# GNN layer pair: places double-buffered, running counts in SBUF, scatters by half groups with a wait in the middle

## The chip, the cores and the metric

One core of a Trainium2 chip runs the whole program. The metric is the device time of one launch in microseconds, without a profile. The kernel before has a median of 7398.5 us over three runs. A profile is taken in an execution of its own, which is slower: see the section on the profile.

## The reference

Two graph layers over 12500 nodes of 128 features and 212500 directed edges (`src`, `dst`, sorted by `dst`), each followed by a residual and a layer norm:

```python
# layer 0
h = silu(edge_attr @ W1 + b1)
messages = x[dst] * (h @ W2 + b2)
aggregated = segment_sum(messages, src, 12500)
x = layernorm(x + concat(x @ Wself + bself, aggregated) @ Wcat + bcat)
# layer 1
a_in  = mean over dst of (x @ W_in.T + b_in)[src]
a_out = mean over src of (x @ W_out.T + b_out)[dst]
x = layernorm(x + gru_cell(concat(a_in, a_out), x))
```

In layer 0 the messages are made in the order of `dst` and summed by `src`. The kernel therefore sorts them: it works out for each edge its place in the order of `src`, and scatters each message to its row of the DRAM tensor `msgs`.

## The kernel before

Edges are worked on in 208 groups of 1024 (`NG` = 208, `GE` = 1024), each group as `TG` = 8 tiles of 128. After a preamble (144.3 us in the trace) the edge phase runs over the groups in pairs (`b` = 0, 1 are the two buffers of a pair); then `sums0` adds up the scattered messages by blocks, the first layer norm follows, and then layer 1 with 3322 gathers of 128 rows each (L757), issued by GpSimd; last comes the GRU cell with the second norm.

The edge phase is the stage that the change touches. Every engine has its own instruction stream with waits on semaphores written by hand. In group g:

- SP (L475 to L494) loads rows of keys, attributes and a window of x.
- PE: for both halves of the group, the neighbours' rows by a one-hot product (`neighbours`, L1827) for g, the hidden layer (`hidden`, L1820) and the transposed attributes (`attributes`, L1814) for g+1. Then `places(g)` (L1836): eight products of `place` with a column of ones, which give the place of each edge, into `places_at`, a strip of PSUM bank 7. Then `weights` (L1842, L1844) in two halves, and the first half of the attributes of g+2, ahead of which PE waits for `pos_ready`, that is until DVE has copied the places of g; the attributes share bank 7 with the places.
- DVE: one-hots of the source digit (L1337) and the attribute parts (L1364 to L1367) of a later group, then for g+1 the running counts by a scan (`running_counts`, L1344) into `so_far`, which is PSUM bank 6, and the product of counts and one-hots (`places_of`, L1351) into `place` in SBUF, each twice, once per half, with the window's one-hots (L1373) between. `place` has one buffer, so the first product waits until PE's `places(g)` is done (`place_ready`). Then DVE copies the places of g to `pos` (L1398; it waits for `place_ready` and for the scatters of g-2) and multiplies weights and neighbours to messages, in two halves (L1379), into `mrow`.
- ACT: copies out of PSUM (L856, L858, L870), the activation (L864) and the two key columns of `mrow` (L886, L887).
- GpSimd (`scatters`, L697): waits for `pos_ready`, `key_ready` and both halves of `msg_ready`, and then issues eight indirect DMAs, one per tile, of 128 rows of 544 bytes, from `mrow` to `msgs`. `mrow` and `pos` have two buffers; the semaphores `scattered[b]` count the landings, 16 per DMA.

`Steps.wait` (L65) is a wait of DVE for its own last instruction; `hold` (L85, L86) is a wait of GpSimd and a nop behind it.

Of the kernel before, what the change touches and what calls it, by code (L numbers as in the profile page):

```python
# [8 lines left out]
P = 128  # L9
TG = 8  # L10
GE = TG * P
NG = -(-E // GE)
# [76 lines left out]
def gnn_kernel(nc, x, src, dst, edge_attr, W1, b1, W2, b2, Wself, bself, Wcat, bcat,  # L89
# [24 lines left out]
    with ctx:  # L114
# [85 lines left out]
        ht = cut(2 * 2 * 4 * P).rearrange("p (b h e) -> p b h e", b=2, h=2)  # L200
        place = cut(GE)
        attr_t = cut(GE, bf16)
        ustage = acc_b[:, 2 * QE + T:2 * QE + T + 3 * SB * D].rearrange("p (h n d) -> p h n d", h=3, n=SB)
        xpart_x = cut(D)
        xpart_t = cut(P)
        xpart_sb = cut(D)

        cut = cutter(arena, STAGE)
# [129 lines left out]
        bank = [ctx.enter_context(nc.psum_tensor(f"bank{i}", [P, 512], f32)) for i in range(8)]  # L338
        so_far = bank[6][:, :]
        attr_at = bank[7][0:W1R, 0:2 * P].bitcast(bf16)  # L340
        places_at = bank[7][:, 2 * P:2 * P + TG]
        xpart_at = bank[7][:, 2 * P + TG:3 * P + TG]

# [286 lines left out]
        def _(pool):  # L630
# [59 lines left out]
            def scatters(it):  # L690
                for b in range(2):
                    g = 2 * it + b
                    hold(pool, s["pos_ready"], g + 1)
                    hold(pool, s["key_ready"], 2 * g + 2)
                    hold(pool, s["msg_ready"], 2 * g + 2)
                    for j in range(TG):
                        pool.indirect_dma_start(msgs, bass.IndirectOffsetOnAxis(ap=pos[:, b, j:j + 1], axis=0), mrow[:, b, j, :], None).then_inc(scattered[b], 16)  # L697

# [374 lines left out]
        def _(dve):  # L1073
# [272 lines left out]
            def places_of(stp, g, b, h):  # L1346

                stp.wait()
                need(dve, s["place_ready"], 0 if h else g)
                half = oht[:, b, 4 * h:4 * h + 4, :].rearrange("p j e -> p (j e)")  # L1350
                stp.mark(v.tensor_tensor(place[:, h * 4 * P:(h + 1) * 4 * P], so_far, half, ALU.mult))  # L1351
                if h:
                    stp.wait()
                    dve.sem_inc(s["place_in"], 1)
# [70 lines left out]
            v.tensor_copy(blk0_f, blk0[:, :]).then_inc(s["blk0_copied"], 1)  # L1425
            v.memset(acc_a[:, :], 0.0)
            us.link(v.tensor_copy(node_at, iota_row[:, :]))
            def onehot0(q, k):
# [260 lines left out]
        def _(pe):  # L1689
# [111 lines left out]
            def attributes(g, b, h, nb=None):  # L1801

                pe.wait_ge(s["attr_cut"], g + 1)
                need(pe, s["attr_sb"], 2 * g + h)
                if h == 0:
                    need(pe, s["pos_ready"], g - 1)
                if nb is not None and b:
                    mm(xpart_at, ones_b[0:3, :], bias3[:, :], start=True, stop=False)
                    mm(xpart_at, xpart_t, wcomb[:, :], start=False, stop=True)
                elif nb is not None:  # L1810
                    pe.wait_ge(x_staged[0], nb * 16 + 16)
                    tr(xpart_at, xpart_x, ident[:, :])
                for k in range(4):
                    last = tr(attr_at[:, k * P:(k + 1) * P], attr_p[:, b, 4 * h + k, :, :].rearrange("p k c -> p (k c)"), ident_b[:, :])  # L1814
                last.then_inc(s["attr_tr"], 1)
# [14 lines left out]

            def places(g):

                pe.wait_ge(s["place_in"], g + 1)
                need(pe, s["pos_ready"], g)
                for j in range(TG):
                    last = mm(places_at[:, j:j + 1], place[0:NBP, j * P:(j + 1) * P], ones[0:NBP, 0:1], start=True, stop=True)  # L1836
                last.then_inc(s["place_ready"], 1)
# [9 lines left out]
            def edge_group(it, more=True, nb=None):  # L1847
                for b in range(2):
# [9 lines left out]
                    if then:  # L1858
                        hidden(g + 1, 1)
                    places(g)  # L1860
                    for h in range(2):
# [147 lines left out]
```

## Time and profile before

| | |
|---|---|
| median of 3 runs (lowest, highest) | 7398.5 us (7398.36, 7406.37) |
| profiled execution, its own span | 9306.0 us, granted TensorE clock 0.655 |
| edge phase in it, first to last scatter | 3255.0 us |
| first to last gather in it | 5002.2 us |
| GpSimd busy | 5138.4 us of the span |
| PE, DVE, ACT busy | 4988.0, 3928.4, 1905.1 us |

The span runs from the first to the last instruction of the profiled execution; the runs of the first line have no profile. A timeline row of GpSimd's DMA_INDIRECT shows how long the engine works on issuing the DMA, not its landing. In brackets behind a row stands how long the engine was idle before it and what ended that; "issue" means that no wait was found, "remote" that a semaphore's update ended the wait whose origin the profile doesn't find among the instructions near it. Ends of matmuls are modelled.

### The profile page before, as it was taken

The page shows a single profiled execution, that of the slowest core. Times are in us where ns is not written, and L with a number is a line of the kernel's source. Part 1 is how long each engine was busy: PE and PEld are TensorE (multiplying, and loading weights), DVE is VectorE, ACT ScalarE, POOL GpSimd, SP SyncE. Part 2 cuts the span into 40 slices and gives each one's busy share as a digit, 9 for nine tenths or more (in the row PEclk, how much of TensorE's full clock was granted, in tenths as well). Part 3 has the DMA queues.
Part 4 walks back from the last instruction along what each step waited for, and adds up shares of the span by engine and source line. Part 5 has one row for each costly group of instructions (what it writes and reads, how often), then busy time and mean ns, then how long its engine had stood idle before and what let it go on. Part 6 is the DMA issues. An engine that isn't in the chain of part 4 may idle for free. (4 is left out here: it accounts for less than half of the span.)

```text
span 9306.0 us, 123877 instructions
## 1 busy us (share of the span) xinstructions
PE 4988.0 (54%) x25826; PEld 4200.2 (45%) x25826; DVE 3928.4 (42%) x9767; ACT 1905.1 (20%) x6476; POOL 5138.4 (55%) x5753
## 2 busy tenths in 40 slices
PE   5777777767677778833323333333344444434438
PEld 4666666666666668823222232222232333222334
DVE  6444444444445467743222242232332222222238
ACT  2222222222222210021111111111121111111117
POOL 2454544444445455554666666666556666666651
PEclk7666666666666679966555555555576666666668
DMA  3222222222222248731222212222122222222224
GB/s 101 80 84 77 82 78 78 75 76 77 78 75 82 81 141 229 232 94 34 46 46 47 46 41 46 47 46 46 39 53 60 60 60 61 60 59 60 61 67 147
DMA packets 947495, 711.24 MB, mean 76 GB/s; under 512 B 602499, under 2 KB 811606, under 8 KB 946622
## 3 DMA queue, kind: packets, MB, share of 16 engines
q0 software_dynamic: 163632, 347.28, 12.5%
q1 hardware_dynamic: 245634, 251.14, 8.9%
q10 hardware_dynamic: 538001, 110.77, 6.2%
q14 instruction: 205, 1.68, 0.1%
q8 instruction: 23, 0.38, 0.0%
HBM read 544.79 MB, written 170.29 MB: 77 GB/s over the span
## 5 line engine op out<-in xcount | busy, mean ns | idle before, releaser
L757 POOL DMA_INDIRECT arena<-x1d,edge x3322 | 3147.5, 947 | 1859.2 <-issue 957.7
L1937 PE MATMUL bank<-arena 128*128 x7040 | 1433.8, 381 | 2159.8 <-DVE acc_b L1585 1129.5
L697 POOL DMA_INDIRECT msgs<-arena x1664 | 1618.8, 973 | 1761.4 <-DVE arena L1379 1290.2
L1937 PEld LDWEIGHTS bank<-arena 128*128 128x128 f32 x7040 | 1310.9, 285 | 2354.6 <-issue 2345.0
L1579 DVE TENSOR_TENSOR arena<-bank,arena 128x1024 f32<-128x1024 f32 x440 | 537.5, 1222 | 2518.7 <-remote 2182.8
L987 ACT ACTIVATE arena<-edge,arena 128x1 f32 x3520 | 730.3, 282 | 2600.0 <-issue 2021.4
L1351 DVE TENSOR_TENSOR acc_b<-bank,arena 128x512 f32<-128x512 f32 x416 | 287.6, 691 | 1474.5 <-remote 1368.0
L1585 DVE TENSOR_TENSOR acc_b<-acc_b,bank 128x129 f32 x1760 | 507.2, 288 | 661.5 <-issue 467.3
L1844 PE MATMUL bank<-w2s,acc_b 128*128 128x128 f32 x3328 | 739.6, 392 | 0.0
L1827 PE MATMUL bank<-arena 128*128 (+1 forms) x3328 | 729.1, 389 | 1.0 <-DVE arena L1373 0.6
L1844 PEld LDWEIGHTS bank<-w2s,acc_b 128*128 128x128 f32 x3328 | 628.9, 282 | 134.9 <-issue 134.9
L1827 PEld LDWEIGHTS bank<-arena 128*128 128x128 f32 x3328 | 663.1, 295 | 2.1 <-issue 1.1
L1585 DVE TENSOR_TENSOR acc_a<-acc_a,bank 128x129 f32 x1760 | 507.2, 288 | 280.0 <-issue 82.0
L1891 PE MATMUL bank<-arena 128*128 128x128 f32 x3712 | 500.1, 300 | 86.4 <-DVE acc_a L1450 63.3
L1344 DVE TENSOR_TENSOR_SCAN bank<-arena,bank 128x512 f32<-128x512 bf16 x415 | 535.4, 1290 | 7.3
L1891 PEld LDWEIGHTS bank<-arena 128*128 128x128 f32 x3712 | 487.8, 203 | 98.7 <-DVE acc_a L1450 69.2
L1923 PE MATMUL bank<-auxw,arena 9*128 9x512 bf16 x98 | 56.2, 574 | 860.6 <-ACT arena L981 837.9
L856 ACT ACTIVATE acc_b<-bank 128x128 f32<-128x128 f32 x196 | 54.3, 277 | 2031.5 <-PE bank L1814 1838.3
L1836 PEld LDWEIGHTS bank<-ones,acc_b 99*128 99x128 f32 x3328 | 454.3, 211 | 11.3
L1836 PE MATMUL bank<-ones,acc_b 99*128 99x1 f32 x3328 | 425.3, 257 | 0.0
L1923 PEld LDWEIGHTS bank<-auxw,arena 9*128 9x128 bf16 x98 | 9.6, 98 | 879.5 <-ACT arena L981 854.7
L713 POOL TENSOR_SCALAR arena<-iota_row,arena 128x128 f32<-128x128 f32 x464 | 273.3, 601 | 195.8 <-PE bank L1891 195.2
(310 smaller groups left out, 5591.1 us busy)
## 6 DMA issues: line engine op xcount, KB each, us to landing
arena<-rows SPq DMA_DIRECT2D x208, 512.0 KB
arena<-msgs ACTq DMA_DIRECT2D x464, 136.0 KB, 3.2
arena<-msgs SPq DMA_DIRECT2D x464, 136.0 KB, 3.0
arena<-x1d,edge POOLq DMA_INDIRECT x3322
msgs<-arena POOLq DMA_INDIRECT x1664
pred<-arena ACTq DMA_DIRECT2D x98, 256.0 KB
arena<-pred SPq DMA_DIRECT2D x12, 1792.0 KB, 8.8
arena<-xwin SPq DMA_DIRECT2D x208, 64.0 KB
```

The costliest lines, as they stand in the source:

```text
L697: pool.indirect_dma_start(msgs, bass.IndirectOffsetOnAxis(ap=pos[:, b, j:j + 1], axis=0), mrow[:, b, j, :], None).then_inc(scattered[b], 16)
L757: pool.indirect_dma_start(grow_t[:, sl, 0:D], None, x1d, bass.IndirectOffsetOnAxis(ap=edge2[:, odd * RING + sl, 1:2].bitcast(i32), axis=0) ...
L987: last_key = nc.scalar.activation(key_now[:, slot, k:k + 1], edge2_f[:, bass.ds(of[k], 1)], ACT.Identity, bias=blk_now[:, slot, k:k + 1])
L1344: stp.mark(v.tensor_tensor_scan(so_far, half, before_it.to_broadcast([P, 4 * P]), before_it, ALU.add, ALU.max))
L1351: stp.mark(v.tensor_tensor(place[:, h * 4 * P:(h + 1) * 4 * P], so_far, half, ALU.mult))
L1579: v.tensor_tensor(oh1[:, q % 2], node_at.rearrange("p (o n) -> p o n", o=1).to_broadcast([P, TG, P]), key_now[:, slot, q * TG:(q + 1) * TG ...
L1585: v.tensor_tensor(a, a, sum_at(q, k), ALU.add).then_inc(s["add1_done"], 1)
L1827: last = mm(bank[4 + h][:, k * P:(k + 1) * P], wsel[:, b, j, :], win[:, b, bass.ds(wide * j, 1), :].rearrange("p o d -> p (o d)"), start=T ...
L1836: last = mm(places_at[:, j:j + 1], place[0:NBP, j * P:(j + 1) * P], ones[0:NBP, 0:1], start=True, stop=True)
L1844: last = mm(bank[2 + h][:, k * P:(k + 1) * P], ht[:, b, h, k * P:(k + 1) * P], w2s[:, :], start=False, stop=(k == 3))
L1891: last = mm(bank[k % 4][:, 0:P], mtile[:, k % S0, i, 0:D], oh0[:, k % SO, i, :], start=(i == 0), stop=(i == 1))
L1937: last = mm(sum_at(q, k), oh1[:, q % 2, k, :], grow[:, bass.ds(rows_at[q * TG + k], CW)], start=True, stop=True)
```

## The change

`place` gets a second buffer, so that DVE's product for g+1 waits for the places of g-1 (`place_ready` at least g, no longer g+1). `so_far` moves from PSUM bank 6 to SBUF, `places_at` moves from bank 7 to bank 6, and PE's wait for `pos_ready` ahead of the attributes goes (the one in `places` stays). GpSimd issues the first four scatters of a group when the first half of the messages is there; before the fifth it waits for the second half and then until the group's first four scatters have landed. A wait of DVE for the last `pos_ready` is added once, behind the loop, before bank 6 is written for other use.

```diff
@@ -198,12 +198,13 @@
 
         cut = cutter(acc_b[:, 2 * QE + T:NBP * CW], NBP * CW - 2 * QE - T)
         ht = cut(2 * 2 * 4 * P).rearrange("p (b h e) -> p b h e", b=2, h=2)
-        place = cut(GE)
+        place = cut(2 * GE).rearrange("p (b e) -> p b e", b=2)
         attr_t = cut(GE, bf16)
         ustage = acc_b[:, 2 * QE + T:2 * QE + T + 3 * SB * D].rearrange("p (h n d) -> p h n d", h=3, n=SB)
         xpart_x = cut(D)
         xpart_t = cut(P)
         xpart_sb = cut(D)
+        so_far = cut(4 * P)
 
         cut = cutter(arena, STAGE)
         S0, SO = NS, 8
@@ -336,10 +337,9 @@
         part_sum = sb("part_sum", [P, 2, LO])
 
         bank = [ctx.enter_context(nc.psum_tensor(f"bank{i}", [P, 512], f32)) for i in range(8)]
-        so_far = bank[6][:, :]
         attr_at = bank[7][0:W1R, 0:2 * P].bitcast(bf16)
-        places_at = bank[7][:, 2 * P:2 * P + TG]
-        xpart_at = bank[7][:, 2 * P + TG:3 * P + TG]
+        places_at = bank[6][:, 0:TG]
+        xpart_at = bank[7][:, 2 * P:3 * P]
 
 
         names = """pads_oh0 pool_const edges_in weights_in dve_step pe_weights act_weights dve_weights aux_in
@@ -692,8 +692,11 @@
                     g = 2 * it + b
                     hold(pool, s["pos_ready"], g + 1)
                     hold(pool, s["key_ready"], 2 * g + 2)
-                    hold(pool, s["msg_ready"], 2 * g + 2)
                     for j in range(TG):
+                        if j % 4 == 0:
+                            hold(pool, s["msg_ready"], 2 * g + 1 + j // 4)
+                        if j == 4:
+                            hold(pool, scattered[b], it * (16 * TG) + 16 * 4)
                         pool.indirect_dma_start(msgs, bass.IndirectOffsetOnAxis(ap=pos[:, b, j:j + 1], axis=0), mrow[:, b, j, :], None).then_inc(scattered[b], 16)
 
             with pool.Fori(0, NG // 2) as it:
@@ -1346,9 +1349,9 @@
             def places_of(stp, g, b, h):
 
                 stp.wait()
-                need(dve, s["place_ready"], 0 if h else g)
+                need(dve, s["place_ready"], 0 if h else g - 1)
                 half = oht[:, b, 4 * h:4 * h + 4, :].rearrange("p j e -> p (j e)")
-                stp.mark(v.tensor_tensor(place[:, h * 4 * P:(h + 1) * 4 * P], so_far, half, ALU.mult))
+                stp.mark(v.tensor_tensor(place[:, b, h * 4 * P:(h + 1) * 4 * P], so_far, half, ALU.mult))
                 if h:
                     stp.wait()
                     dve.sem_inc(s["place_in"], 1)
@@ -1424,6 +1427,7 @@
             dve.wait_ge(s["dlist_out"], 16)
             v.tensor_copy(blk0_f, blk0[:, :]).then_inc(s["blk0_copied"], 1)
             v.memset(acc_a[:, :], 0.0)
+            dve.wait_ge(s["pos_ready"], NG)
             us.link(v.tensor_copy(node_at, iota_row[:, :]))
             def onehot0(q, k):
                 v.tensor_tensor(oh0[:, (4 * q + k) % SO], node_at.rearrange("p (o n) -> p o n", o=1).to_broadcast([P, 2, P]),
@@ -1802,8 +1806,6 @@
 
                 pe.wait_ge(s["attr_cut"], g + 1)
                 need(pe, s["attr_sb"], 2 * g + h)
-                if h == 0:
-                    need(pe, s["pos_ready"], g - 1)
                 if nb is not None and b:
                     mm(xpart_at, ones_b[0:3, :], bias3[:, :], start=True, stop=False)
                     mm(xpart_at, xpart_t, wcomb[:, :], start=False, stop=True)
@@ -1828,12 +1830,12 @@
                               win[:, b, bass.ds(wide * j, 1), :].rearrange("p o d -> p (o d)"), start=True, stop=True)
                 last.then_inc(s["xj_ready"], 1)
 
-            def places(g):
+            def places(g, b):
 
                 pe.wait_ge(s["place_in"], g + 1)
                 need(pe, s["pos_ready"], g)
                 for j in range(TG):
-                    last = mm(places_at[:, j:j + 1], place[0:NBP, j * P:(j + 1) * P], ones[0:NBP, 0:1], start=True, stop=True)
+                    last = mm(places_at[:, j:j + 1], place[0:NBP, b, j * P:(j + 1) * P], ones[0:NBP, 0:1], start=True, stop=True)
                 last.then_inc(s["place_ready"], 1)
 
             def weights(g, b, h):
@@ -1857,7 +1859,7 @@
                     neighbours(g, b, 1)
                     if then:
                         hidden(g + 1, 1)
-                    places(g)
+                    places(g, b)
                     for h in range(2):
                         weights(g, b, h)
                     if more:
```

## Rows read from the trace of the kernel before

**Rows 1.** The page's head: span of the profiled execution and its instructions.

```profile
span 9306.0 us, 123877 instructions
```

**Rows 2.** Windows: edge phase and gathers; columns PE, PEld, DVE, ACT, POOL busy, clock, DMA.

```profile
core 0: us, PE busy (x) PEld busy (x) DVE busy (x) ACT busy (x) POOL busy (x), PEclk, DMA share, GB/s
...
144.30:3399.30 3255.00, 2369.82 (x12793) 2045.79 (x12791) 1562.79 (x2677) 781.68 (x1847) 1618.81 (x1664) 0.64 0.24 79
...
4038.10:9040.30 5002.20, 1805.13 (x7856) 1452.37 (x7856) 1543.32 (x3995) 875.24 (x3834) 3147.51 (x3322) 0.61 0.22 52
```

**Rows 3.** Waits of GpSimd: line, releaser, us in total, times, longest in us.

```profile
POOL msgs L697 <- DVE arena L1379: 1290.2, 207, 125.2
POOL arena L757 <- issue: 957.7, 3140, 0.9
POOL arena L757 <- remote: 663.3, 164, 5.5
POOL msgs L697 <- issue: 470.0, 1453, 2.2
POOL arena L757 <- PE bank L1937: 233.6, 17, 90.6
```

**Rows 4.** Waits in the edge phase, same columns: DVE's place product.

```profile
DVE acc_b L1351 <- remote: 1368.0, 175, 8.9
```

**Rows 5.** Timeline of GpSimd, one group's scatters and the next group's first.

```profile
start us, us, engine line op out<-in xcount [idle before <-releaser]
1502.09 0.97 POOL L697 DMA_INDIRECT msgs<-arena  x1 [6.94 <-DVE arena L1379]
1503.36 0.97 POOL L697 DMA_INDIRECT msgs<-arena  x1 [0.30 <-issue]
1504.63 1.02 POOL L697 DMA_INDIRECT msgs<-arena  x1 [0.30 <-issue]
1505.96 0.97 POOL L697 DMA_INDIRECT msgs<-arena  x1 [0.30 <-issue]
...
1511.04 0.97 POOL L697 DMA_INDIRECT msgs<-arena  x1 [0.30 <-issue]
1518.85 0.97 POOL L697 DMA_INDIRECT msgs<-arena  x1 [6.84 <-DVE arena L1379]
```

**Rows 6.** Timeline of DVE in the same stretch.

```profile
1502.45 0.36 DVE L1367 TENSOR_TENSOR arena<-arena 128x192 bf16<-128x192 f32 x1
...
1503.92 0.89 DVE L1373 TENSOR_SCALAR arena<-arena,iota_c 128x1024 f32<-128x1024 bf16 x1
1513.62 0.69 DVE L1351 TENSOR_TENSOR acc_b<-bank,arena 128x512 f32<-128x512 f32 x1 [8.81 <-remote]
...
1516.59 0.17 DVE L1398 CAST arena<-bank 128x8 int32<-128x8 f32 x1 [0.22 <-DVE acc_b L1351]
1516.78 1.29 DVE L1379 TENSOR_TENSOR arena<-bank,arena 128x512 f32<-128x512 f32 x2
```

**Rows 7.** Timeline of PE in the same stretch: places and the second weights.

```profile
1505.84 1.94 PE L1836 MATMUL bank<-ones,acc_b 99*128 99x1 f32 x16
...
1509.42 2.07 PE L1844 MATMUL bank<-w2s,acc_b 128*128 128x128 f32 x8
```

**Rows 8.** Timeline at the edge phase's end: last scatter, first load behind all scatters.

```profile
3398.33 0.96 POOL L697 DMA_INDIRECT msgs<-arena  x1 [0.31 <-issue]
3400.80 1.42 ACTq L918 DMA_DIRECT2D arena<-msgs  x3
```

**Rows 9.** Timeline around a gap in a group's scatters, DVE and GpSimd.

```profile
347.83 0.17 DVE L1398 CAST arena<-bank 128x8 int32<-128x8 f32 x1 [0.24 <-DVE acc_b L1351]
...
353.29 0.97 POOL L697 DMA_INDIRECT msgs<-arena  x1 [2.23 <-issue]
...
355.36 0.69 DVE L1351 TENSOR_TENSOR acc_b<-bank,arena 128x512 f32<-128x512 f32 x1 [2.70 <-PE bank L1836]
...
358.33 0.17 DVE L1398 CAST arena<-bank 128x8 int32<-128x8 f32 x1 [0.22 <-issue]
```

## The prediction, made before the changed kernel was run

> **What bounds the kernel now.** I read the profile in this order: the span, the split of GpSimd's time by stretch, GpSimd's waits, and then one turn of the edge loop engine by engine. The profiled execution spans 9306.0 us [rows 1]; the runs without a profile have a median of 7398.5 us. The two differ by 1907.5 us, so before any cost is added up the reader has to ask which of the waits in the trace exist in the timed runs at all.
>
> The edge loop takes 3255.0 us for 208 groups (15.65 us each), and the gathers 5002.2 us [rows 2]. In both GpSimd issues indirect DMAs one after another. GpSimd's waits account for its edge time exactly: 1618.8 us busy, 470.0 us of gaps between DMAs ("issue"), and 1290.2 us of waiting for the messages, of which 125.2 us is one wait ahead of the loop, so 1165.0 us inside [rows 2, 3]. In the gathers it waits 663.3 us for something that the profile can't name, and 233.6 us for PE, of which 90.6 us in one place [rows 3].
>
> Where the 1165.0 us come from is to be seen in one turn. GpSimd issues the eight scatters of a group at 1.27 us a piece, the first at 1502.09 and the last at 1511.04 [rows 5]. PE's records end early: the products that give the places (L1836) start at 1505.84 and last 1.94 us, the second half of the message products starts at 1509.42 and lasts 2.07 us [rows 7]. Yet DVE's place product (L1351), which needs the semaphore of exactly that L1836, starts only at 1513.62 after 8.81 us of idling [rows 6], 2.58 us after the last scatter began. In 175 groups DVE so waits, 1368.0 us in all [rows 4]. PE's completions thus come late while GpSimd issues, and everything behind them (counts, places, messages, the next scatters at 1518.85) goes in a row. The Trainium skill (Perfetto Trace Analysis, "Per-instruction lifecycle: what the profiler-reported window actually captures") says that a matmul's end is computed from its size, not observed. So the record's end doesn't contradict the late semaphore; no term below rests on this.
>
> Do the timed runs have those waits? Take away from the profiled span the 1165.0 us and the 663.3 us: 7477.7 us. The median is 79.2 us less still, which is 0.016 us for each of the 4986 indirect DMAs. I read from this that in the timed runs GpSimd hardly waits, and that the late completions belong mostly to the profiled execution. Then a group costs GpSimd (1618.8 + 470.0) / 208 = 10.04 us, and GpSimd sets the pace. One caution: a turn without the late completion took 358.33 - 347.83 = 10.50 us from one copy of the places to the next [rows 9], a little over 10.04. So PE and DVE in turn are nearly as slow, and PE's busy time is 2369.8 / 208 = 11.4 us a group at a granted clock of 0.64 [rows 2], mostly the 1.2 GHz level. In the timed runs they must be near or under GpSimd's 10.04 or the median couldn't be that low.
>
> **The change part by part.** The sum is made per group, times 208, and put onto the median, since the profiled execution has waits that I hold to be its own.
>
> *The place buffer twice, counts in SBUF, places in a bank of their own.* DVE's product for group g+1 now needs the places of g-1 and not of g; PE's attribute transposes no longer wait for the copy of the places (pos_ready). In the turn shown this takes product, scan and product out of the path, from 1513.62 to 1516.59, 2.97 us [rows 6]. Where GpSimd is the bound this is worth nothing: what is late next is GpSimd itself. Queued behind the copy on DVE are the two message products, as before. The work added is none; DVE has 1562.8 / 208 = 7.5 us of work per group [rows 2], so a few hundredths from another source or destination memory lie beside GpSimd's scatters. Bounds: 0 and -2.97 us per group.
>
> *A rule that speaks against it.* The product now reads the counts from SBUF, as well as the one-hots. The existing product of two SBUF inputs, L1367 (1502.45, 0.36 us), ran while the scatter of 1502.09 was being issued, and that scatter took 0.97 us like its neighbours; the conversion L1373 (1503.92), with one input, is the one beside which a scatter took 1.02 us [rows 5, 6]. The Trainium skill (SBUF — State Buffer, "Who interferes with whom") says that a DVE instruction with two SBUF inputs contends with a GpSimd instruction that reads SBUF. By the row the cost is 0. By the rule, if it blocked the scatters for the two products of 0.69 us, it would be 1.38 us per group, 287 us in all; the trace doesn't show it.
>
> *Scatters by half groups.* The first four need only the first half of the messages. DVE makes the two halves in 1.29 us together from 1516.78 [rows 6], so the first four may start some 0.6 us earlier when GpSimd waits for messages. When GpSimd is the bound: 0. Bounds 0 and -0.6 us.
>
> *The fifth scatter waits until the first four have landed.* This is the term that counts. GpSimd's queue is in order: behind the wait stand scatters five to eight and the whole next group. It can't be free: the fourth scatter alone is at work for 0.97 us, and the next began 1.27 us after its start [rows 5]. What the trace shows of landing: the last scatter started at 3398.33, and the first load that waits for all scatters was issued at 3400.80, 2.47 us later [rows 8]. From the wait's end to a scatter's start: the second message product ended at 1516.78 + 1.29 = 1518.07, the scatter began at 1518.85, 0.78 us later [rows 5, 6]. Together 3.25 us from fourth to fifth start; from below it is 0.97 + 0.78 = 1.75. Against the usual 1.27 that is 1.98 or 0.48 us more. I take 1.7, close to the upper end, because 2.47 is the same DMA and the same kind of wait, less some tenths for the loading engine's own first instruction. Nothing on GpSimd covers it. What can is only slack that the group has now, if PE and DVE at 10.50 and not GpSimd at 10.04 set the pace: I take 0.3 us off for that, more than half of the difference.
>
> Sum: 208 x (1.7 - 0.3) = 291 us, 7398.5 + 291 = 7690 us. A group goes from 10.04 to about 11.7 us, and that is also above PE's 11.4. The profiled execution may well go the other way: with a pause in a train of scatters PE's completions came in time. After the gap of 2.23 us ahead of the scatter of 353.29 DVE's product ran at 355.36 already, on a wait of 2.70 us [rows 9]. There the group would fall from 15.65 to some 12.3 us and the span to about 8600 us.
>
> **The rivals.**
>
> *The pause is covered.* If PE's clock in the timed runs is as low as in the trace, PE's 11.4 us is the pace now. The indirect DMAs must then be shorter for the median to come out: by (79.2 + 208 x 1.36) / 4986 = 0.073 us, a train 9.45 us. With the pause 11.15 us, still under 11.4; with the waits of PE on DVE gone, the gain is 0 to 0.3 us a group: 7340 to 7400 us, and up to 7600 with half the slack. For it: PE's busy time. Against: it needs shorter DMAs than any row.
>
> *The late completions are in the timed runs too.* This is the case on the other side. The 957.7 and 470.0 us of "issue" gaps [rows 3] might be the profiler's instead; without them the span is 7878 us, so 480 of the 1828 us of waits would be gone and 1349 stay, of which the edge loop's share 860 us, 4.1 us a group. Then the change pays: 2.97 + 0.6 us leave the path, 1.7 come in, -1.9 us x 208 = -390 us: about 7010 us; if the pause also lets PE's completions through, down to 6800. It decides from 1.7 us of wait per group on. For it: waits are measured, the gap's origin isn't. Against: it needs all 0.30 us gaps to vanish, where the other reading meets the median within 1%.
>
> *More than the pause.* Landing at the full 1.98 us with no slack is 412 us, 7810 us; with the rule of the ports above (a chance of 0.02) near 8000.
>
> That the change doesn't do what it says is excluded: a fourth scatter that works for 0.97 us can't have landed when the fifth is due after 0.30.
>
> **How the numbers follow.** Forecast 0.54 (7600 to 7790); pause covered 0.18, a third each faster, equal and slower; late completions real 0.18; more than the pause 0.10. A measurement of this kernel can tell about 0.2% (15 us) from no change. Faster: 0.18 + 0.06 = 0.24; same 0.06; slower 0.54 + 0.10 + 0.06 = 0.70. The forecast's own range is 7600 to 7790. To hold 8 in 10 the range takes in the covered pause, the near end of the gain and the exposed pause in full: 7250 to 7820.
>
> **What would show it.** In the changed kernel's trace: the fifth scatter (L697's successor) starts about 3.0 us after the fourth, the others 1.27; if under 2, my main term is wrong. DVE's product no longer waits for PE; in its place the copy of the places or the message products wait. PE's completion is late in fewer groups and by less. The edge stretch is near 2560 us, the other stretches are unchanged. A scatter over 1.0 us beside L1351 would speak for the port rule. If the median falls by over 15 us, the reading that the timed runs have no GpSimd waits is wrong, and with it the sum.

## The result and the profile after

| | before | changed | ratio, 95% interval |
|---|---|---|---|
| first comparison, median | 7398.43 us | 7797.49 us | 1.0542 [1.0529, 1.0555] |
| second, chip 11 | 7382.4 us | 7799.31 us | 1.0566 [1.0548, 1.0584] |
| third, chip 10 | 7390.66 us | 7804.93 us | 1.0555 [1.0533, 1.0577] |

The change makes the kernel 5.5% slower, 399 us in the first comparison. It was predicted as slower, 7690 us, with a range of 7250 to 7820 us. (For the first comparison the record gives no number of the chip.)

One thing has to be known to understand every number below. The kernel before runs in two ways, and all its runs on one chip went the same way: in 7382 to 7398 us (medians) in three comparisons, in 9254 to 9331 us in three others. The trace ahead of the prediction (9306.0 us) is of the second kind, the times beside it are of the first. I call the chips quick and late; whether it is the chip, or a state that it was in at the time, isn't known. A comparison is always made within one chip.

The changed kernel's profiled execution spans 7803.8 us, and its time was 7805.69 us: it was on a quick chip, and its time is within 0.3% of the other three runs (7784.22 to 7797.62 us), so the trace describes the timed runs; being traced costs next to nothing, other than the section on the metric says. The windows, by stage (columns as in [rows 2]: PE, PEld, DVE, ACT, POOL busy, clock, DMA); edge phase, sums and norm, gathers, end:

```profile
145.30:2798.40 2653.10, 2271.79 (x12789) 1972.87 (x12786) 1537.55 (x2680) 804.49 (x1847) 1735.70 (x1664) 0.72 0.29 96
2798.40:3438.70 640.30, 545.87 (x3908) 523.40 (x3908) 496.11 (x1958) 45.49 (x100) 326.87 (x711) 0.91 0.76 223
3438.70:7601.30 4162.60, 1870.70 (x8048) 1604.27 (x8048) 1597.96 (x4105) 829.58 (x3914) 3150.05 (x3322) 0.64 0.28 62
7601.30:7803.80 202.50, 171.96 (x718) 98.95 (x718) 174.28 (x841) 160.50 (x585) 28.06 (x19) 0.93 0.60 192
```

The edge phase takes 2653.1 us, 12.76 us a group, against 15.65 in [rows 2]; but the gathers, which the change doesn't touch, take 4162.6 us against 5002.2. So the two traces can't simply be subtracted. GpSimd's waits (line, releaser, us, times, longest), which answer to [rows 3]:

```profile
POOL arena L760 <- issue: 1005.2, 3298, 0.3
POOL msgs L700 <- issue: 471.4, 1455, 3.8
POOL msgs L700 <- DMA msgs<-arena: 445.9, 208, 3.4
POOL msgs L700 <- DVE arena L1382: 126.3, 1, 126.3
```

GpSimd no longer waits for messages, apart from the once ahead of the loop. It waits 445.9 us, 208 times, for the landing of its own scatters: the new wait. GpSimd's timeline from the fourth scatter of one group to the sixth of the next, with the fifth scatter of each (1504.52 and 1517.61) behind 2.15 and 2.41 us of idling where [rows 5] has 0.30:

```profile
1501.23 1.14 POOL L700 DMA_INDIRECT msgs<-arena  x1 [0.30 <-issue]
1504.52 1.54 POOL L700 DMA_INDIRECT msgs<-arena  x1 [2.15 <-DMA msgs<-arena]
1506.37 0.97 POOL L700 DMA_INDIRECT msgs<-arena  x1 [0.30 <-issue]
1507.64 0.96 POOL L700 DMA_INDIRECT msgs<-arena  x1 [0.30 <-issue]
1508.91 0.96 POOL L700 DMA_INDIRECT msgs<-arena  x1 [0.30 <-issue]
1510.18 0.97 POOL L700 DMA_INDIRECT msgs<-arena  x1 [0.30 <-issue]
...
1514.22 0.99 POOL L700 DMA_INDIRECT msgs<-arena  x1 [0.30 <-issue]
1517.61 1.29 POOL L700 DMA_INDIRECT msgs<-arena  x1 [2.41 <-DMA msgs<-arena]
1519.20 0.97 POOL L700 DMA_INDIRECT msgs<-arena  x1 [0.30 <-issue]
```

The next group's first scatter (1510.18) follows the last of this one (1508.91) after the usual 0.30 us: the queue of GpSimd is full from end to end, and what is put into it lengthens the phase.

A second effect stands in the same rows. The fifth scatters take 1.54 and 1.29 us, not 0.97. DVE at that time:

```profile
1504.01 1.28 DVE L1347 TENSOR_TENSOR_SCAN acc_b<-arena,acc_b 128x512 f32<-128x512 bf16 x1
1505.33 0.69 DVE L1354 TENSOR_TENSOR acc_b<-acc_b,arena 128x512 f32<-128x512 f32 x1
1511.21 0.17 DVE L1401 CAST arena<-bank 128x8 int32<-128x8 f32 x1 [5.20 <-DMA msgs<-arena]
...
1516.84 1.28 DVE L1347 TENSOR_TENSOR_SCAN acc_b<-arena,acc_b 128x512 f32<-128x512 bf16 x1
1518.16 0.69 DVE L1354 TENSOR_TENSOR acc_b<-acc_b,arena 128x512 f32<-128x512 f32 x1
```

The second place product ends at 1505.33 + 0.69 = 1506.02 and the scatter at 1506.06; in the next group the product ends at 1518.85 and the scatter at 1518.90. Without being held the scatters would have ended at 1505.49 and 1518.58. The product has both inputs in SBUF now. Ahead of the copy of the places (1511.21) DVE idles 5.20 us, until the scatters of two groups before have landed and their buffer is free: DVE waits for GpSimd, not GpSimd for DVE, so PE and DVE don't set the pace of the changed kernel. The group of all scatters on the page is 70 ns longer in the mean than the 973 ns of the kernel before:

```profile
L700 POOL DMA_INDIRECT msgs<-arena x1664 | 1735.7, 1043 | 1043.7 <-issue 471.4
```

### The profile page after: what moved, and what is told of

The parts are those of the page before. It is cut to its first block, busy times and chain, and to the rows that moved or that the text cites. A ratio compares the mean times of both kernels' runs of the same rounds, so it can differ in the third digit from the quotient of the medians.

```text
span 7803.8 us, 124501 instructions
## 1 busy us (share of the span) xinstructions
PE 4919.8 (63%) x25826; PEld 4245.4 (54%) x25826; DVE 3916.0 (50%) x9767; ACT 1867.1 (24%) x6476; POOL 5257.6 (67%) x5753
## 4 chain that ended last, share of the span: by engine, by line
POOL 38%; issue 13%; PE 7%; DVE 2%; ACT 1%; DMA 1%; DVEq 1%; POOLq 0%; ACTq 0%; SPq 0%
POOL arena L760 38%; PE bank L1893 6%; PE bank L1939 1%; DVEq L405 1%; DMA arena<-x1d,edge 1%; ACT acc_a L946 0%; ACT acc_b L946 0%; DMA edge<-dlist 0%; DVE acc_a L1454 0%; PE bank L1986 0%; DVE arena L1659 0%; POOLq L85 0%; DVE arena L1667 0%; DVE some_mv L1474 0%; DVE arena L1583 0%
## 5 line engine op out<-in xcount | busy, mean ns | idle before, releaser
L1939 PE MATMUL bank<-arena 128*128 x7040 | 1566.7, 411 | 2256.8 <-SPq L579 1565.3
L700 POOL DMA_INDIRECT msgs<-arena x1664 | 1735.7, 1043 | 1043.7 <-issue 471.4
L990 ACT ACTIVATE arena<-edge,arena 128x1 f32 x3520 | 677.6, 280 | 2034.9 <-issue 1932.8
L1829 PE MATMUL bank<-arena 128*128 (+1 forms) x3328 | 613.4, 342 | 0.1
L1347 DVE TENSOR_TENSOR_SCAN acc_b<-arena,acc_b 128x512 f32<-128x512 bf16 x415 | 531.7, 1281 | 7.5
L1838 PEld LDWEIGHTS bank<-ones,acc_b 99*128 99x128 f32 x3328 | 524.1, 240 | 8.4
L1838 PE MATMUL bank<-ones,acc_b 99*128 99x1 f32 x3328 | 494.3, 278 | 0.0
L889 ACT ACTIVATE arena<-arena 128x8 f32 (+1 forms) x208 | 45.1, 217 | 1612.0 <-DMA msgs<-arena 1612.0
L1822 PE MATMUL bank<-acc_b,arena 96*128 96x512 bf16 x416 | 196.6, 472 | 355.3 <-ACT acc_b L861 353.9
L1433 DVE TENSOR_TENSOR arena<-bank,arena 128x256 f32<-128x256 f32 x696 | 290.9, 418 | 82.3 <-issue 67.5
```

The source lines that it names most:

```text
L990: last_key = nc.scalar.activation(key_now[:, slot, k:k + 1], edge2_f[:, bass.ds(of[k], 1)], ACT.Identity, bias=blk_now[:, slot, k:k + 1])
L1347: stp.mark(v.tensor_tensor_scan(so_far, half, before_it.to_broadcast([P, 4 * P]), before_it, ALU.add, ALU.max))
L1433: v.tensor_tensor(oh0[:, (4 * q + k) % SO], node_at.rearrange("p (o n) -> p o n", o=1).to_broadcast([P, 2, P]), local[:, q % 2, k, :].rear ...
L1829: last = mm(bank[4 + h][:, k * P:(k + 1) * P], wsel[:, b, j, :], win[:, b, bass.ds(wide * j, 1), :].rearrange("p o d -> p (o d)"), start=T ...
L1838: last = mm(places_at[:, j:j + 1], place[0:NBP, b, j * P:(j + 1) * P], ones[0:NBP, 0:1], start=True, stop=True)
L1939: last = mm(sum_at(q, k), oh1[:, q % 2, k, :], grow[:, bass.ds(rows_at[q * TG + k], CW)], start=True, stop=True)
```

## The experiments

The theory: GpSimd's queue is the bound on a quick chip, the wait lengthens it by what lies between the fourth scatter and its landing, and nothing covers it. The rivals: the counts in SBUF cost most of the loss; or PE and DVE set the pace. Quick and late chips came up as the runs went on.

### What a late chip is: the kernel before, traced again

No edit. 

> The kernel before, profiled once more. Question: are the late PE completions (1165 us of GpSimd's waits for messages in the edge phase, 663 us in the gathers) a property of a profiled execution of this kernel, or of that one execution? The changed kernel's profile had none of them in either phase, although the change touches the edge phase alone. Theory A (a passing state of that execution): span near 7400 us, edge phase 2250 us (10.8 us a group), gathers about 4160 us, GpSimd waiting under 150 us for messages. Theory B (this kernel, when it is profiled, always falls into it): span near 9300 us, edge phase 3250 us.

Measured: 9270.36 us, and in seven other runs of the kernel before on the same chip 9254.39 us (9219.99 to 9303.13). Waits:

```profile
POOL msgs L697 <- DVE arena L1379: 1282.5, 207, 125.7
POOL arena L757 <- remote: 630.7, 156, 5.2
POOL msgs L697 <- issue: 470.6, 1455, 2.2
```

These are [rows 3] again. The numbers are those of theory B, but its reason is wrong: the waits are no property of profiling, since the timed runs are as slow.

The trace also records when a semaphore was updated, which shows the lateness for the whole loop. In the trace of [rows 5 to 7] the update of `place_ready` comes 5.6 us (median) after the modelled end of the group's last L1836, and over 0.5 us after it in 191 of 208 groups. In the trace of the kernel without the wait on a quick chip (below) it comes 0.014 us after it, and in no group over 0.02 us. DVE's updates behind the messages come 0.01 us (median) after their end in the late trace too. Records of ACT's updates are too incomplete there to tell.

A second time on another chip:

> The kernel before, for its trace where it is fast (the only traces of it so far are of executions of 9268 and 9306 us). If before takes some 7390 us here: GpSimd's waits for messages are 0.3 to 0.9 us a group (10.80 us a group from the times, of which 7.75 busy and 2.35 usual gaps leave 0.7), the scatters' mean is 0.97 us, the gathers take 4160 us. If it takes some 9250 us, the trace is like the first.

Measured: 9247.82 us, seven other runs beside it 9330.71 us (9301.8 to 9379.25). So the kernel before has no trace on a quick chip.

### The changed kernel without the wait

```diff
-                        if j == 4:
-                            hold(pool, scattered[b], it * (16 * TG) + 16 * 4)
```

The wait guards no data, so the kernel is complete without it. 

> The changed kernel without the wait for the first four landings. Theory 1 (the pause is the main term, 2.15 us of gap ahead of the fifth scatter where 0.30 is usual, and the scatters that run beside the place products and scans cost another 0.6 us a group): a group takes 8 x 0.97 + 0.6 + 8 x 0.30 = 10.8 us, the median 7380 to 7420 us, no different from before. Rival 2 (the pause is all, the longer scatters come from it): about 10.2 us a group, 7260 to 7300 us. Rival 3 (the move of the counts to SBUF is what costs): 7600 us or more.

Measured on a late chip: 8769.01 us, ratio to before 0.9476 [0.9434, 0.9517]. None of the three expectations had a late chip in it, and none can be judged by this run. It was run twice more:

> The changed kernel without the wait. Where before takes 7390 us. Theory 1 (pause 1.85 us a group; 0.6 us from scatters beside products with both inputs in SBUF): 10.1 + 0.6 = 10.7 us a group, 7370 to 7400 us. Rival 2 (no such lengthening without the pause): 10.2 us a group, 7260 to 7300 us. Rival 3 (the counts in SBUF cost more than the pause): 7600 us or more. Where before takes 9250 us: 8770 us again.

> The changed kernel without the wait, a third time: on two chips the kernel before took 9254 and 9331 us and this one 8769 and 8847; on a third the kernel before took 7382 us and the changed one 7799. Where before takes some 7390 us here. Theory 1 (pause 1.85 us a group, the rest of the loss from scatters beside products with both inputs in SBUF): 7370 to 7420 us, ratio 0.995 to 1.005. Rival 2 (the scatters lengthen only with the pause): 7260 to 7300 us, ratio 0.985. Rival 3 (counts in SBUF cost most of the loss): 7600 us or more. Where before takes 9250 us or more: ratio 0.945 to 0.95.

Both came to late chips: 8847.01 us, ratio 0.9464 [0.9431, 0.9497], and 8765.8 us, ratio 0.9473 [0.9414, 0.9532]. On a late chip this part of the change alone makes the kernel 5.3% faster; the ratio agrees over the three chips, while 8847.01 us misses the expected 8770 by as much as that chip's kernel before is longer. The trace of the first of the three runs (8769.01 us) says how. GpSimd's wait for messages, then DVE's timeline:

```profile
POOL msgs L698 <- DVE arena L1380: 743.3, 195, 124.8
```

```profile
1507.32 0.69 DVE L1352 TENSOR_TENSOR acc_b<-acc_b,arena 128x512 f32<-128x512 f32 x1
1511.69 0.17 DVE L1399 CAST arena<-bank 128x8 int32<-128x8 f32 x1 [3.68 <-PE bank L1836]
1513.18 0.69 DVE L1380 TENSOR_TENSOR arena<-bank,arena 128x512 f32<-128x512 f32 x1 [1.32 <-PE bank L1844]
1515.40 0.69 DVE L1380 TENSOR_TENSOR arena<-bank,arena 128x512 f32<-128x512 f32 x1 [1.52 <-PE bank L1844]
```

PE's completion of the places is still late (the last L1836 ends at 1510.60 by its record, 1.09 us before the copy starts), but the product, scan and product are done at 1508.01, before it comes; the copy follows it at once, where in [rows 6] it stood 2.97 us behind. GpSimd's waits for messages fall from 1282.5 - 125.7 = 1156.8 us to 618.5 us.

### Both on one quick chip: the verdict on the wait

> The changed kernel, beside the same without the wait, on one chip: so far the two were never on the same one. The kernel before is either at 7390 us (a quick chip) or at 9250 to 9330 us (PE's completions late while GpSimd issues). Theory 1: the pause takes 1.85 us more in GpSimd's queue and puts the fifth scatter beside the second place product, whose two inputs in SBUF hold it up until the product's end, 0.4 us a group. On a quick chip 7800 us. On a slow one GpSimd waits for messages anyway, and the pause lets late completions through: 208 x (13.24 - 12.9) under the kernel without the wait or the same, 8600 to 8800 us, ratio 0.93 to 0.95. Rival: on a slow chip the pause adds in full to the kernel without it: 9150 us, ratio 0.99.

> The changed kernel without the wait, on the same chip as the run with it. Theory 1 on a quick chip: 10.7 us a group, 7370 to 7420 us: the whole loss of the change is the wait and what it moves. Rival 2 on a quick chip: 7260 to 7300 us. Rival 3 on a quick chip (counts in SBUF, not the wait): 7600 us or more. On a slow chip 8770 to 8850 us, ratio 0.947.

Measured, same chip: with the wait 7804.93 us, without it 7394.18 us, the kernel before 7390.66 us; the ratio of the kernel without the wait to before is 1.0009 [0.9995, 1.0023]. Theory 1 holds, rival 2 (7260 to 7300) and rival 3 (7600 or more) fall. **Without the wait the whole loss is gone; the rest of the change, taken together, makes no difference on a quick chip.** It doesn't follow that each part of the rest is worth nothing: see the account of the prediction. Waits with, and then without:

```profile
POOL msgs L700 <- issue: 468.6, 1455, 3.4
POOL msgs L700 <- DMA msgs<-arena: 448.3, 208, 4.0
POOL msgs L700 <- DVE arena L1382: 127.3, 1, 127.3
```

```profile
POOL msgs L698 <- issue: 495.6, 1547, 3.3
POOL msgs L698 <- DVE arena L1380: 149.9, 79, 126.1
POOL msgs L698 <- DVE arena L1399: 7.3, 24, 0.3
```

Inside the loop GpSimd idles 468.6 + 448.3 = 916.9 us with the wait, and 495.6 + (149.9 - 126.1) + 7.3 = 526.7 us without: 390.2 us, 1.88 us a group. Its scatters are busy 1737.9 and 1707.7 us, in the groups by line:

```profile
L700 POOL DMA_INDIRECT msgs<-arena x1664 | 1737.9, 1044 | 1044.2 <-issue 468.6 <-DMA msgs<-arena 448.3 <-DVE arena L1382 127.3
```

```profile
L698 POOL DMA_INDIRECT msgs<-arena x1664 | 1707.7, 1026 | 657.1 <-issue 495.6 <-DVE arena L1380 149.9 <-DVE arena L1399 7.3
```

That is another 30.2 us, 0.15 us a group. Together 420 us in the trace; the medians differ by 410.8 us.

### The kernel before with the wait alone

```diff
                     for j in range(TG):
+                        if j == 4:
+                            hold(pool, scattered[b], it * (16 * TG) + 16 * 4)
```

> The kernel before with nothing but the wait ahead of the fifth scatter. Theory 1: GpSimd is the bound and nothing covers the pause: 10.1 + 1.85 = 11.95 us a group plus what GpSimd waits for messages now (before: 10.8 - 10.1 = 0.7, which the pause may cover): 7640 to 7780 us, somewhat under the changed kernel's 7797, since no scatter runs beside a product with two SBUF inputs. Rival 3 (counts in SBUF cost, the pause is covered): 7400 to 7500 us.

> The kernel before with the wait alone. Where before takes 7390 us. Theory 1: nothing covers the pause on GpSimd, 1.85 us a group = 385 us at the most, less what GpSimd waited for messages in the kernel before: 7640 to 7780 us. Rival 3 (the pause is covered): 7400 to 7500 us. Where before takes 9250 us: 8950 us again.

Both runs were on late chips: 8951.71 us, ratio 0.9673 [0.9626, 0.9719], and 9044.83 us, ratio 0.9677 [0.9641, 0.9712]; the second misses the expected 8950 us, again on the chip whose kernel before is longer. There the wait alone makes the kernel 3.3% faster. Waits on GpSimd, then its timeline and DVE's:

```profile
POOL msgs L699 <- DVE arena L1381: 530.1, 90, 127.3
POOL msgs L699 <- issue: 450.6, 1362, 2.2
POOL msgs L699 <- DMA msgs<-arena: 449.7, 204, 4.7
```

```profile
1516.52 0.97 POOL L699 DMA_INDIRECT msgs<-arena  x1 [0.30 <-issue]
1519.58 0.97 POOL L699 DMA_INDIRECT msgs<-arena  x1 [2.08 <-DMA msgs<-arena]
```

```profile
1518.40 0.69 DVE L1353 TENSOR_TENSOR acc_b<-bank,arena 128x512 f32<-128x512 f32 x1 [3.02 <-remote]
```

GpSimd pays 449.7 us for landings, of which some 60 us would have been usual gaps, and waits 402.8 us for messages instead of 1156.8. In the pause PE's completion of the places arrives: DVE's product starts at 1518.40, in the 2.08 us in which GpSimd is idle, not after the group's last scatter. The start is still 2.09 us behind the modelled end of the places' products (1516.31). The fifth scatter takes 0.97 us here, with the counts in PSUM. On a quick chip this kernel wasn't run, so the wait's price is shown there in the changed kernel alone.

### Counts in PSUM: the price of the port

The changed kernel without the wait, and with the counts, the places and PE's wait for their copy as in the kernel before:

```diff
-        so_far = cut(4 * P)
...
+        so_far = bank[6][:, :]
         attr_at = bank[7][0:W1R, 0:2 * P].bitcast(bf16)
-        places_at = bank[6][:, 0:TG]
-        xpart_at = bank[7][:, 2 * P:3 * P]
+        places_at = bank[7][:, 2 * P:2 * P + TG]
+        xpart_at = bank[7][:, 2 * P + TG:3 * P + TG]
...
+                if h == 0:
+                    need(pe, s["pos_ready"], g - 1)
```

> The places twice and the scatters by halves, but the running counts stay in PSUM bank 6, the places in bank 7 with PE's wait for their copy, and there is no wait for landings. It differs from the changed kernel without the wait only in where the counts and the places lie. Theory 1 (scatters are lengthened by DVE's product with both inputs in SBUF): the scatters' mean falls back from 1.04 to 0.97 us, a group takes 10.1 to 10.3 us, the median is 7260 to 7310 us, 1.2 to 1.9% under the kernel before. Rival 4 (PE and DVE in turn set the pace of a group, not GpSimd): 7390 to 7420 us, as before.

> Places twice, scatters by halves, counts in PSUM, no wait. Where before takes 7390 us. Theory 1 (products with both inputs in SBUF lengthen scatters): scatters' mean 0.97 us, 10.1 to 10.3 us a group, 7260 to 7310 us, under both before and the changed kernel without the wait. Rival 4 (PE and DVE set the pace in the kernel before, and here): 7370 to 7400 us. Where before takes 9250 us: 8810 us again.

Late chips both, and the second longer than the expected 8810 us like its kernel before: 8810.95 us, ratio 0.9522 [0.9482, 0.9563], beside 8769.01 with the counts in SBUF; and 8845.43 us, ratio 0.9467 [0.9434, 0.9501], beside 8847.01. The first pair differs by 42 us, the second not at all, so the times don't settle which is quicker on a late chip. The scatters tell them apart; counts in SBUF, then in PSUM, on the same chip:

```profile
L698 POOL DMA_INDIRECT msgs<-arena x1664 | 1659.7, 997 | 1218.1 <-DVE arena L1380 743.3 <-issue 472.9 <-DVE arena L1399 1.8
```

```profile
L698 POOL DMA_INDIRECT msgs<-arena x1664 | 1640.3, 986 | 1275.0 <-DVE arena L1380 798.5 <-issue 476.2 <-DVE arena L1399 0.3
```

19 us less, and 27 us less on the second chip (1636.3 against 1663.0). It doesn't fall back to the 973 ns of the kernel before, so the expectation of 0.97 us for the mean was missed.

The mean hides how clear the effect is, since most scatters meet no product in the moment that counts. Take the same moment in both traces, a group's second product that starts 0.8 us after a scatter. First with the counts in SBUF, GpSimd and then DVE:

```profile
330.05 1.55 POOL L698 DMA_INDIRECT msgs<-arena  x1 [0.30 <-issue]
```

```profile
330.86 0.69 DVE L1352 TENSOR_TENSOR acc_b<-acc_b,arena 128x512 f32<-128x512 f32 x1
```

Then with the counts in PSUM:

```profile
330.88 0.97 POOL L698 DMA_INDIRECT msgs<-arena  x1 [0.30 <-issue]
```

```profile
331.70 0.69 DVE L1352 TENSOR_TENSOR acc_b<-bank,arena 128x512 f32<-128x512 f32 x1
```

This holds over the whole phase. All 12 such scatters with the counts in SBUF took 1.55 to 1.56 us, all 48 with the counts in PSUM 0.97. In the late trace of the kernel before, 150 scatters overlap a product, and each took 0.96 to 0.97 us. So a product lengthens a scatter only with the counts in SBUF; where the work of DVE falls decides how often. (The edit moves the places too, but the product reads only the counts and the one-hots.) What this kernel does on a quick chip, where GpSimd is the bound and where it was expected under the kernel before, stays open.

### The changed kernel on a second chip

> The changed kernel itself once more, beside the kernel before on the same chip. The kernel before took 7398 us when the change was measured, and 9254 us, without a profile too, on the chip of the four runs before this one, with the late PE completions of the first trace. So the late completions are a property of a chip (or of its state) and not of profiling. Theory 1: if before takes some 9250 us here, the changed kernel is FASTER than before: the pause costs 1.85 us a group as in the wait alone, and the earlier products gain at least the 2.3 us a group by which the kernel without the wait was faster; the wait alone gained 1.5 us there. I expect 8600 to 8900 us, ratio 0.93 to 0.96. Rival: where completions are late the pause adds to the kernel without the wait, 8769 + 208 x 1.85 = 9150 us, ratio 0.99. If before takes some 7400 us here, both theories say 7780 to 7810 us again.

Measured: 7799.31 us beside 7382.4 us, a quick chip, as expected for that case. The case for which it was run, a late chip, didn't come: the changed kernel was never run on one. Whether it wins or loses there isn't known; its two halves win alone (0.947 and 0.967), and how they add wasn't measured.

Nor is it known what makes a chip late. Of six comparisons three were quick (the first, chips 11 and 10) and three late (chips 6, 2 and 3), and no chip is known to have come twice. In the three quick ones the changed kernel took part and in the late ones it didn't. The kernel before was quick or late together with the others, in its own untouched runs, and a cause in the company of kernels isn't excluded.

## Why the prediction was right, and where it wasn't

The direction, the main term and the stated range held: a group's fifth scatter starts 3.10 us (median) after the fourth, where about 3.0 was announced, and DVE's copy waits in place of its product. The changed kernel's 7797 us lies 23 us inside the range's upper end. How the sum came about is less good than that, as follows.

**What bounds the kernel.** "GpSimd hardly waits in the timed runs, and sets the pace": right. The changed kernel's queue has no gap for messages, and without the wait the groups take 2238.7 / 208 = 10.76 us with 24 us of waits for messages in all 208. The reason given for it was wrong. The late completions don't belong to the profiled execution; they are there in timed runs of 9254 us. They go with late chips, and by its times the first trace must come from one, though the record doesn't name it. The sum of 9306.0 - 1165.0 - 663.3 = 7477.7 us against 7398.5 was close by luck, because errors of both signs met, as the windows of the kernel without the wait show (edge phase, gathers, end):

```profile
144.70:2383.40 2238.70, 2040.81 (x12794) 1765.66 (x12792) 1547.15 (x2680) 803.39 (x1848) 1707.69 (x1664) 0.79 0.36 114
...
3024.10:7187.60 4163.50, 1874.47 (x8048) 1607.73 (x8048) 1597.07 (x4105) 830.24 (x3914) 3151.55 (x3322) 0.64 0.28 62
7187.60:7390.60 203.00, 172.53 (x718) 99.37 (x718) 174.63 (x841) 160.71 (x585) 28.10 (x20) 0.92 0.59 191
```

The edge phase is 149 us longer than the 2090 us that the subtraction left, the gathers 175 us shorter than 4338.9 (their 233.6 us of waiting for PE went as well, which I had left in), the end 63 us shorter. That is for the kernel without the wait, whose time is that of the kernel before; the kernel before itself has no such trace. So a changed group takes 12.76 us and not the 11.7 of the sum, mostly because it starts from some 10.7 us and not from 10.04.

**The pause.** Taken as 1.7 us between bounds of 0.48 and 1.98. Measured: 2.15 us of idling where 0.30 is usual (448.3 / 208 = 2.16), so 1.85 us, and 1.88 over all gaps. From fourth to fifth start it was 3.10 us in the median (3.29 in the rows above, whose fourth scatter took 1.14) against a bound of 3.25. The term was undersized by 0.15 to 0.18 us a group, 31 to 37 us.

**The slack of 0.3 us.** In the changed kernel nothing covers the pause: without the wait GpSimd idles 1.88 us less a group, and the time falls by all of it. Booked against the kernel without the wait, this step failed by 62 us. Whether the kernel before had slack is another question, and no run answers it, since it has no trace on a quick chip. An estimate: outside the edge phase it is the same program as the kernel without the wait, whose edge phase takes 2238.7 us and whose median is 3.5 us higher. Then its own edge phase takes some 2235 us on a quick chip. Its scatters and usual gaps took 1618.8 + 470.0 us in the late trace, which leaves 146 us of waiting for messages, 0.7 us a group. The kernel without the wait has 24 us of that.

**Places twice, halves: "worth nothing where GpSimd is the bound".** Right as a net on a quick chip, 1.0009, but by the same estimate not as reasoned. Some 120 us of waits for messages went, 33 of them came back as usual gaps and waits for the places, and the scatters grew by 1707.7 - 1618.8 = 89 us: a gain and a loss of the same size. This stays an estimate, because the 1618.8 is from a late chip. On late chips the 2.97 us came off the path as described, and gave 5.3%.

**The port rule.** It was given a chance of 0.02 and no cost. The row it was set aside by, L1367 beside a scatter of 0.97 us, was no test: the product of 0.36 us was over 0.25 us before the scatter ended. The second place product of a group outlasts the scatter's usual 0.97 us and holds it until its own end, as the rows above show. The Trainium skill (SBUF — State Buffer, "Who interferes with whom") says that a DVE instruction with two SBUF inputs contends with a GpSimd instruction that reads SBUF; by this, the trace agrees for the second product. The same section of the Trainium skill infers that a `tensor_tensor` leaves the making of a DMA's descriptors on GpSimd alone; with the indirect scatters held to 1.54 and 1.29 us the trace doesn't agree with that. Between the kernels with and without the wait the scatters differ by 0.15 us a group (30.2 us). Against the kernel before it is more, 1737.9 - 1618.8 = 119 us or 0.57 us a group, with the same reservation. It isn't the 1.38 us of the worst case: the first product of a group, right behind the conversion of the window's one-hots, held hardly any. In the trace of the first late run without the wait it started 0.60 to 0.65 us after a scatter 151 times, and each of these scatters took 0.96 to 0.98 us and ended 0.35 to 0.36 us before the product.

Two bookings of the miss are possible. Against the kernel without the wait: pause 34, slack 62 and scatters 30 us, together 126 where the forecast missed by 107. Against the kernel before, by the estimate: the pause costs 448.3 us less 208 usual gaps of 0.30 us (62.4), 386 us (354 were taken); the scatters cost 119 (0 were taken); and of the 146 us of waits for messages the part beyond the usual gaps, 84 us, goes (62 were taken as slack). That is 421 us; the traced executions are a little further apart than the medians. By the first booking the slack is the step that failed, by the second the port that was put at nothing, and the slack was about right. Only a trace of the kernel before on a quick chip could decide. Both have the pause as the main term and undersized. So the time came out as the rival "more than the pause" had it (7810 us), though not wholly for its reason; the forecast's own range, which ended at 7790, was 7 us too low.

**The rival on the other side** ("late completions are in the timed runs too", 6800 to 7010 us at a chance of 0.18) was wrong for the times that the case is measured by, and right as a mechanism: on a late chip the wait alone gains 3.3%, because the pause lets PE's completions through, which the prediction had read from the turn of [rows 9].

## What to carry to other kernels

A span of the profile that is 26% over the median isn't a detail of profiling: ask for the times of the very chip that was traced before any wait in the trace is called real or unreal. Where one engine's queue is full from end to end, a wait put into it costs its full length, here 1.85 us x 208; take it from the nearest row of landing, and take off slack only where a row of the same state shows it. A buffer moved into SBUF can lengthen another engine's work without adding any of its own: test it by a row in which the two end together, not by one in which the first is over long before. A net of zero from several edits isn't a zero for each. And a remedy found in one trace can be a loss on the chips that don't have the disease.

## What the runs showed of the hardware

- On some chips PE's semaphores come late while GpSimd issues indirect DMAs one after another: in [rows 5, 6] DVE's wait ends at 1513.62, 1.6 us after the issue of the last scatter has ended at 1512.01. GpSimd's DMAs themselves are no slower there (0.97 us, every 1.27). The update of `place_ready` comes 5.6 us (median) after the modelled end there, and 0.014 us in a trace from a quick chip. The kernel before takes 25% longer where they do, 9254 us against 7382 to 7398.
- A gap of about 2 us in the train can let them through: in the kernel before with the wait alone DVE's product started inside a pause of 2.08 us (1518.40), and in [rows 9], after a gap of 2.23 us, the product started 0.39 us after the modelled end of the places' products (354.97 in that trace). It isn't enough in every group, since 402.8 us of waits for messages were left.
- A group's second place product with both inputs in SBUF holds a scatter that is being issued until 0.05 us after its own end, if it outlasts the scatter's usual 0.97 us: 1.55 us in all 12 meetings 0.8 us after the scatter's start. With the counts in PSUM it never does (48 such meetings, 0.97 us).
- A scatter's issue is also held by the conversion of the window's one-hots, which has one input in SBUF, but this too depends on where the counts lie. In the kernel without the wait, on a quick chip, the scatter of 1518.70 ended at 1520.45, 0.12 us after the end of L1374 (timelines of GpSimd and of DVE):

```profile
1518.70 1.75 POOL L698 DMA_INDIRECT msgs<-arena  x1 [0.30 <-issue]
```

```profile
1519.60 0.73 DVE L1374 TENSOR_SCALAR arena<-arena,iota_c 128x1024 f32<-128x1024 bf16 x1
```

  It isn't the order in which the two start that decides. In [rows 6] a conversion started at 1503.92 as well, 0.56 us after the scatter of 1503.36 [rows 5], and that scatter took its 0.97 us. On one chip (6), of the conversions that started 0.5 us or more after the start of a scatter still in its 0.97 us, all 34 held it with the counts in SBUF (1.40 to 1.78 us), and none of 39 did with the counts in PSUM (at most 1.01 us). The operation right ahead of the conversion is the scan that writes the counts, and its target is what differs; why that matters, no run shows. Over the phase the scatters take 1707.7 us here against 1618.8 in the kernel before on a late chip, 0.43 us a group. That the kernel without the wait is no slower fits the waits for messages that it no longer has, by the estimate above.
